# Turning the second slot group one routed step later, and the first group's second product and copy ahead of the next group's work

## What is computed

```python
x = layernorm(x + mamba2(x, ...))            # projections, conv, scan, gate, out projection
gates = softmax(xf @ router_w)               # 14 routed experts
top_v, top_i = top_k(gates, 2)               # two experts for each token
h = x * rsqrt(mean(x * x) + RMS_EPS) * rw    # for each expert
routed = silu(h @ W1) @ W2                   # W1 128x256, W2 256x128, for each routed expert
out = einsum(routed, masked gates) + shared  # two shared experts for every token
x = layernorm(x + out)
```

## Time and profile before

| | us |
|---|---|
| median of 3 runs | 774.05 |
| lowest and highest of them | 773.05, 775.83 |
| the profiled execution | 773.15 |
| its span, first to last instruction | 771.4 |

### The profile page before, as it was taken

How to read it: one execution, slowest core, us unless ns; L and a number is a source line. 1 busy time by engine, 2 the same in 40 slices (tenths; PEclk the granted TensorE clock), 3 DMA queues, 4 the chain that set the end, 5 groups by cost and what they waited for, 6 DMA issues and landing times.

```text
span 771.4 us, 14722 instructions
## 1 busy us (share of the span) xinstructions
PE 647.2 (84%) x4299; PEld 552.6 (72%) x4299; DVE 598.5 (78%) x1758; ACT 443.6 (58%) x1225; POOL 496.2 (64%) x545
## 2 busy tenths in 40 slices
PE   5987798999999999999999989876597868666740
PEld 4765576788888888888888878756597768666740
DVE  4999999999999999999999867238236324588885
ACT  4885687867877876887787544421114111245545
POOL 1144455888788787888878874656665656655661
PEclk9999999999999999999999999988698898998875
DMA  8641111211221121121111055223222223455436
GB/s 304 193 138 40 45 39 37 72 49 60 66 63 61 52 63 56 58 68 59 55 54 62 23 164 172 57 67 93 77 70 79 83 84 107 134 153 155 143 95 218
DMA packets 62638, 70.76 MB, mean 92 GB/s; under 512 B 10335, under 2 KB 45285, under 8 KB 62304
## 3 DMA queue, kind: packets, MB, share of 16 engines
q1 hardware_dynamic: 52656, 52.79, 23.0%
q0 software_dynamic: 8608, 16.87, 6.5%
q10 hardware_dynamic: 1296, 0.16, 0.1%
HBM read 48.55 MB, written 23.01 MB: 93 GB/s over the span
## 4 chain that ended last, share of the span: by engine, by line
PE 51%; DVE 17%; issue 15%; another core or an unknown queue 5%; ACT 5%; DMA 3%; SPq 3%; POOL 1%; DVEq 0%; ACTq 0%; POOLq 0%
PE bank L791 7%; PE bank L800 6%; PE bank L858 5%; PE bank L774 5%; DVE xbcT_area L1118 4%; PE bank L726 4%; DVE decay_area L1126 3%; PE bank L746 3%; PE bank L807 3%; PE bank L855 3%; PE bank L845 3%; PE bank L759 2%; PE bank L862 2%; PE bank L766 2%
## 5 line engine op out<-in xcount | busy, mean ns | idle before, releaser
L600 POOL DMA_INDIRECT returned<-xT,slots_in x141 | 142.1, 1008 | 103.1 <-DVE xT L1412 64.8
L659 POOL DMA_INDIRECT dispatched<-rows,row_u x128 | 145.6, 1138 | 31.6 <-issue 31.4
L1118 DVE SCALAR_TENSOR_TENSOR xbcT_area<-raw,conv_w,xbcT_area 128x512 f32<-128x512 f32 x162 | 125.7, 777 | 3.3 <-ACT xbcT_area L973 3.3
L726 PE MATMUL bank<-xT 128*128 128x128 f32 x564 | 87.0, 308 | 44.8 <-issue 31.1
L726 PEld LDWEIGHTS bank<-xT 128*128 128x128 f32 x564 | 79.7, 219 | 49.7 <-issue 34.8
L918 ACT ACTIVATE raw<-bank 128x512 f32<-128x512 f32 (+1 forms) x71 | 39.7, 588 | 121.9 <-remote 65.4
L1412 DVE COPY xT<-bank 128x512 f32<-128x512 f32 (+1 forms) x36 | 24.4, 677 | 100.2 <-remote 86.4
L746 PE MATMUL bank<-xbcT_area,raw 128*128 x564 | 81.6, 304 | 8.6 <-issue 8.6
L1126 DVE TENSOR_TENSOR_SCAN decay_area<-decay_area,ident_heads 128x512 f32<-128x512 f32 x64 | 85.5, 1336 | 0.0
L746 PEld LDWEIGHTS bank<-xbcT_area,raw 128*128 128x128 f32 x564 | 77.9, 219 | 9.8 <-issue 9.8
L907 ACT ACTIVATE x<-x,shift,rstd 128x128 f32<-128x128 f32 x128 | 59.2, 501 | 36.9 <-issue 36.9
(11 more groups left out here) (229 smaller groups left out, 1509.1 us busy)
## 6 DMA issues: line engine op xcount, KB each, us to landing
decay_area<-decay_rows SPq DMA_DIRECT2D x64, 256.0 KB
slots_in<-dispatched SPq DMA_DIRECT2D x141, 64.5 KB
hid<-returned SPq DMA_DIRECT2D x18, 256.0 KB
xT<-xT_dram SPq DMA_DIRECT2D x8, 512.0 KB, 7.9
x<-x_dram SPq DMA_DIRECT2D x8, 512.0 KB, 7.6
out_dram<-x SPq DMA_DIRECT2D x16, 256.0 KB
xT<-returned SPq DMA_DIRECT2D x14, 256.0 KB
returned<-xT,slots_in POOLq DMA_INDIRECT x141
```

Source lines behind the costliest of these rows:

```text
L600: e.indirect_dma_start(returned, bass.IndirectOffsetOnAxis(ap=slots_in[sb_][:, n, D:ROW].bitcast(U32), axis=0), slots_out[b][:, n * P:(n + ...
L659: e.indirect_dma_start(dispatched, bass.IndirectOffsetOnAxis(ap=row_u[t % 2][:, m:m + 1], axis=0), rows[t % 3][:, k, c4, :], None).then_in ...
L726: mm = e.matmul(bank[:, off:off + P], w1_now[b][:, k * P:(k + 1) * P], slotsT[gr % len(slotsT)][:, n % 4 * P:(n % 4 + 1) * P], start=True, ...
L1118: e.scalar_tensor_tensor(o, r[:, n:n + W], conv_w[:, k, TAPS - 1 - n:TAPS - n], o, ALU.mult, ALU.add).then_inc(S["conv"])
```

## The change

TensorE and VectorE get other orders in three routed steps, and the list of the VectorE banks follows.

- Routed step 0 (`i` = 66): TensorE turns group 0 only. Group 1 is turned in routed step 1 (`i` = 67), behind that step's other work and ahead of the first product of group 0.
- Routed step 2 (`i` = 69, group 0): TensorE makes the second product of group 0 first, and turns group 2 and makes the first product of group 1 behind it. VectorE waits for that second product and copies it out first, and then does group 2's copy (line 1396 after the change, 1389 before) and its four weight copies.
- All other groups keep their order. Nothing is added or taken away: 1795 rows of TensorE's list and 1483 of VectorE's are there before and after.

```diff
-        if n == 0:
-            dve_uses += [("slotsT", gr) for gr in range(2)]
+        if n == 0 or n == 1:
+            dve_uses.append(("slotsT", n))
...
-            dve_uses += [("slotsT", n), ("down", n - 2)]
+            dve_uses += [("down", 0), ("slotsT", 2)] if n == 2 else [("slotsT", n), ("down", n - 2)]
...
-            def routed_group(gr):
+            def next_groups(gr):
                 if gr + 2 < GROUPS:
                     turn_slots(gr + 2)
                 if gr + 1 < GROUPS:
                     for n2 in pairs_of(gr + 1):
                         routed_hidden(n2)
+
+            def routed_group(gr):
+
+                if gr > 0:
+                    next_groups(gr)
...
                 mm.then_inc(S["routed_down"])
+                if gr == 0:
+                    next_groups(gr)
...
                 if n == 0:
-                    for gr in range(2):
-                        turn_slots(gr)
+                    turn_slots(0)
                 elif n == 1:
+                    turn_slots(1)
                     for n2 in pairs_of(0):
                         routed_hidden(n2)
...
-            def routed_group(gr):
+            def next_group(gr):
                 if gr + 2 < GROUPS:
                     turned(gr + 2)
                     pick_w1(gr + 2)
+
+            def routed_group(gr):
+                if gr > 0:
+                    next_group(gr)
...
                 e.tensor_copy(slots_out[b][:, cols], dve_ring.bank("down", gr)[:, cols]).then_inc(S["routed_out"])
+                if gr == 0:
+                    next_group(gr)
```

## The result

The changed kernel took 776.30 us (median of 20 runs, 774.48 to 778.0) where the kernel before, in 20 runs beside it, took 774.61 (773.05 to 776.42). The ratio is 1.0019, 95% interval 1.0011 to 1.0027: slower by 1.5 us, 0.9 to 2.1. That is within 0.3% and inside the forecast's range of times, but on the other side of no change: the forecast was a shift between -1.6 and +0.1 us. The profiled execution took 775.99 us, its span 774.2.

A forecast was written before the change was run, and what follows sets the result against it. No engine is full; a closed chain of POOL's indirect DMA runs and VectorE's copies bounds the stage. -1.1 us (first run) + 0.7 (step 68 later) = -0.4 on 774.05, say 773.7 us; range 770.6 to 776.4.

The forecast's parts named there:

- Part 2, the gain of 1.1 us: Group 0's copy comes earlier, so POOL's first return starts at 480.43 instead of 481.53 us, bounded by its own DMAs.
- Part 1, the price of the clock: TensorE's slow clock falls on group 0's first product; step 68 ends 0.7 us later, between 0.5 earlier and 1.2 later.
- The reading that the slow clock harmed nobody in the kernel before: Before, the slow stretch hit step 67's work, which had time to spare: the product behind it waited for VectorE anyway.
- The sum at the first return: First run 1.1 us earlier plus step 68 0.7 us later: -0.4 us, ends -1.6 and +0.1.
- The price of part 2, put at nothing: Group 2's turning and copies and group 1's first product come up to 2 us later, covered by 5.5 us slack.
- the gain is caught: Rival: group 3's transposes signalled late, VectorE's five copies delay group 1's copy; total 0 to +1 us; chance 0.18.
- More pairs: Rival: groups 6 and 7 may share a POOL run, 1.5 us less, some 771 us in all; chance 0.17.
- lost pairs: Rival: from 571 us groups stop sharing POOL runs, 0.7 us more each; some 777 us; chance 0.15.
- The shift passes on to the end: Every later POOL run starts from the one before it, so the first run's shift reaches the end unchanged.

The follow-up runs named there:

- after: First trace of the changed kernel as it is; the kernel's median was 776.30 us, ratio 1.0019.
- e2: Kernel before with only group 0's second product and copy put first in routed step 2; 775.55 us, ratio 1.0009.
- e3: Changed kernel with both groups' transposes repeated in step 67 (36 extra) to keep TensorE busy; 773.72 us, ratio 0.9983.
- e13: Changed kernel with one idle GpSimd operation of about 1.0 us behind group 0's returns, on a fourth chip; 729.26 us, ratio 1.0019.
- e15: e3 with GpSimd pauses ahead of all returns but the first and behind those of groups 0 to 3, fourth chip; 755.70 us, ratio 1.0388.
- e16: Changed kernel with GpSimd pauses ahead of all returns but the first and behind those of groups 0 to 3, fourth chip; 758.43 us, ratio 1.0425.
- e17: Changed kernel as it is, once more, on a fifth chip; 772.38 us, ratio 1.0022.
- e18: Kernel before as it is, once more, on the fifth chip; 770.22 us, ratio 0.9998.
- e5: e3 with GpSimd's first return also waiting for a part of VectorE's top-two of that step; 773.56 us, ratio 0.9983.
- e9: Kernel before with two idle GpSimd operations (3.39 us) between VectorE's copy of group 0 and its returns; 778.79 us, ratio 1.0050.
- e1: Kernel before with only group 1's turning moved to step 67; 775.04 us, ratio 0.9991.
- e4: Changed kernel with GpSimd's first return also waiting for a part of VectorE's top-two of that step; 775.25 us, ratio 1.0002.
- e11: e3 with a 1.06 us GpSimd pause ahead of every group's returns and another behind those of groups 0 to 3; 759.73 us, ratio 0.9788.
- e10: Kernel before with a 1.06 us GpSimd pause ahead of every group's returns and another behind those of groups 0 to 3; 760.66 us, ratio 0.9808.
- e14: Kernel before with GpSimd pauses ahead of all returns but the first and behind those of groups 0 to 3, fourth chip; 758.03 us, ratio 1.0413.

## Why the prediction was wrong, and where right

**Part 2, the gain of 1.1 us: right.** The return lies 1.08 us closer behind the residual in after, e2, e3, e13, e15, e16 and e17 (7.50 us each), and GpSimd's own queue is what bounds it, by 0.30 us.

**Part 1, the price of the clock: right in kind, taken a little low.** In one pair of executions it was 49.18 - 47.70 = +1.5 us, beyond the upper end of 1.2. But in that pair the kernel before was lucky: its 47.70 is one of the earliest of its kind. With group 1 turned in step 66 ten traces give 47.53 to 49.33, mean 48.31; as changed, six give 49.09 to 50.00, mean 49.34; with the clock kept up, four give 47.03 to 47.63, mean 47.36. So part 1 costs 1.0 us where the forecast took 0.7, and without a fall of the clock it gains 0.95, more than the 0.5 that the sum had as its end. The reading that the slow clock harmed nobody in the kernel before was wrong as well. Its own first product at 468.69 stands without a wait behind step 67's work, 1.05 us behind the start of VectorE's first weight copy (467.64); in the changed kernel it is 0.37 us (469.68 to 470.05). And in e18 the slow clock lasts until step 67's work is done, and the first product starts at 471.10, 44.50 us behind the mark (426.60 there) where it was 43.44 in the first trace (468.69). The windows of e18:

```profile
466.00:468.50 2.50, 2.50 (x14) 2.50 (x13) 2.30 (x9) 0.38 (x1) 1.64 (x2) 0.50 0.98 403
468.50:471.00 2.50, 2.50 (x10) 1.46 (x10) 1.96 (x6) 0.36 (x1) 0.00 (x0) 0.57 1.10 320
```

The Trainium skill ("TensorE: Matmul & The Clock Gate", section "Why this matters for your kernels") advises against idle gaps of more than some 3 us between bursts of matmuls. The traces agree in part: over the product that came behind the 3.41 us the granted clock was 0.51 (470.00 to 473.60), and where e3 filled the idle stretches it stayed at 1.00. But the fall came at 466.7 us, at the start of the 3.41 us, when TensorE had been idle for 2.06 us and busy for 0.66.

**The sum at the first return** was -0.4, and is -1.08 + 1.03 = -0.05 us.

**The price of part 2, put at nothing: wrong, and this is the step that failed.** The prediction had the later work of groups 1 and 2 covered by a slack of 5.5 us, and every run's period as a constant ("13.2 us for eight DMAs"). It put the return 0.30 us behind the queue's last write itself, and didn't ask what this does to the run: the two writes join it, so that the run starts 2.7 us ahead of the first return. And the slack of 5.5 us was measured from the product's end to a copy that was held back by the run. What counted was what each engine had done before the hold, and that was not slack. VectorE's five copies for group 3 started 2.9 us into the run before (484.39), and behind the run's end in all four traces whose first run has ten DMAs (after, e2, e3, e17). TensorE's second product of group 1 was issued 4.2 us into the run before, and 8.9 (after) and 8.0 us (e17) into it with the change. Price: 15.74 - 13.18 = 2.6 us in the first pair of traces, 14.68 - 13.07 = 1.6 in the second.

**The rival "the gain is caught" named the mechanism that came,** and got a chance of 0.18: group 3's transposes signalled too late, and VectorE's five copies behind the hold and ahead of group 1's copy, 1.6 us later. In e17 just this is the whole loss (group 3's copies at 493.15, group 1's at 494.74). Its size was too small, at most +1 us in all. It counted the transposes 3.1 us into a run of eight. They did come 3.0 us behind the first return (486.49 - 483.45), but the run was then 5.7 us old, because the two writes had joined it; and TensorE's product, caught too, added 0.7 to 0.9 us in the other traces.

**More pairs and lost pairs** did not decide, though the pairs did change. In the trace after, groups 4 and 5 no longer share a run, and group 5's return is 126.8 us behind the mark in place of 122.5. But e17, which lost as much in its total, has the same pairs there as the trace before, and e5, which has after's split, is among the fast ones.

**"The shift passes on to the end": partly.** With the runs cut it held within 0.5 us. e9's delay of 3.4 us cost 3.9 (2.5 to 5.3), but by a new loss on the way. But the changed kernel's second return is 2.95 us later in the first pair and 0.87 in the second, and the end 1.3 and 4.2 us in the same traces, 1.5 and 2.2 us by the totals. The stage from group 1's return to the end took 276.7 us in the trace before and 270.9 in e18, for the same kernel. What decides that, the pairing or the chip, stays open, and so does why e1 alone, 1 us late at the first return, shows nothing of it in its total (0.9976 to 1.0006). So the longer interval is shown; that it is what makes the total longer rests on the 2.2 us between e1 and the changed kernel, and e3 and e5, whose totals are equal with intervals of 15.50 and 13.13, speak against a carry of one for one. That the merged run is the cause of the interval on the slower chips rests on e4 and e5 (cut by a wait, back at 13.1) and on e1 (no merging, 13.2). What holds VectorE and TensorE back in a long run isn't known.

## What to carry to other kernels

Before moving a start earlier on a queue, look at what it will then touch: here 1.1 us gained joined two runs of indirect DMAs and cost 1.6 to 2.6 us. A slack that is measured up to an event which something else holds back is no slack; ask, on each engine in the order of its program, what must be done before the hold begins. One profile of each kernel wasn't enough for a term of 1 us, and the repeats showed its spread of 1.8 us; where a second chip differs by 6%, a tuned pause should be tried on both.

## What had not been expected of the hardware

- On the chips of all runs but e13 to e16, a run of back-to-back indirect DMAs on GpSimd (1.28 us each) slows the others. TensorE's matmuls come with gaps of 0.4 to 1.8 us, the first of them ending 7.2 us into the run that began at 481.53 and 7.9 us into the changed kernel's first, until some 1.5 us behind the run's end. Behind the runs of eight in the trace before, VectorE's next copy started 1.2 to 1.8 us behind the end. In the changed kernel one VectorE instruction got through earlier (492.33, 1.1 us before the end), and in the later stage some gaps came sooner: in the trace after, 3.0 us into a run that began 1.9 us behind another (540.16).
- A pause of 1.06 us every four DMAs all but ended the waits (0.5 us from 560 to 680 us, in place of 29.2) and made the kernel faster by 1.2%, with all runs cut by 1.9%; 0.41 and 0.64 us did not.
- On the fourth chip, 118 of them in a row left GpSimd waiting 0.6 us for VectorE in all, TensorE's second products stood whole in that time, and the kernel before took 727.7 us in place of 770 to 775; there the same pauses made it 4% slower. What differs between the chips is not known.
- The best on the slower chips was e11 (the change with the clock kept up and all runs cut), 759.73 us, and it beats both kernels there; e10 is within its uncertainty. On the fourth chip e14 to e16, which are built alike, are slower than the kernel before by 28 to 31 us.
